# First attention: runs of 320 keys in the traded softmax weights, and another order of their transfers

## The reference, cut to what matters

```
q = (latents @ Wq)                       # latents: layernorm(x), 4 batches x 256 rows
k, v = concat([ctx, latents]) @ Wk, Wv   # 1601 + 256 = 1857 keys, 4 key heads, 8 query heads share one
scores = einsum('bqhgd,bkhd->bhgqk', q, k) / sqrt(128)
attn   = softmax(scores)
out    = einsum('bhgqk,bkhd->bqhgd', attn, v)   # then @ Wo
```

## Time and profile before

| | |
|---|---|
| median of 3 runs | 3167.3 us (3165.0 to 3168.3) |
| the profiled execution, its own time | 3163.8 us |
| its span in the profile | 3162.1 us |
| busy share of the span | PE 95%, PEld 84%, DVE 66%, ACT 56%, POOL 28% |
| granted PE clock, mean | 0.983 |
| softmax part of the first attention | about 545 to 2086 us of the span |

### The profile page before, as it was taken

The page is one execution under the profiler, slowest core; times in us unless marked ns, Lnnn a source line. Parts: engine busy times, 40 slices in busy tenths (PEclk is TensorE's granted clock), DMA queues, the critical chain, the costliest instruction groups (busy, mean ns, idle before and its releaser), DMA issues. The chain is left out here.

```text
span 3162.1 us, 53842 instructions
## 1 busy us (share of the span) xinstructions
PE 3008.4 (95%) x18405; PEld 2670.3 (84%) x18405; DVE 2076.8 (66%) x3217; ACT 1761.0 (56%) x3357; POOL 889.4 (28%) x725
## 2 busy tenths in 40 slices
PE   8999998999999999999999999979979899999886
PEld 8888887799999999899998999978857788888675
DVE  3333333688888888788887888864454466667576
ACT  3322344566766666666666666652243466556363
POOL 0000121344444444344444444442200021111234
PEclk9999999899999999999999999999989899999999
DMA  7665595776777767677767777546746511110387
GB/s 250 215 217 200 200 294 204 146 161 160 164 163 157 162 159 162 152 162 159 160 157 158 159 161 158 138 130 232 237 161 229 182 30 41 33 35 28 124 302 263
DMA packets 395364, 522.17 MB, mean 165 GB/s; under 512 B 35356, under 2 KB 292684, under 8 KB 395112
## 3 DMA queue, kind: packets, MB, share of 16 engines
q1 hardware_dynamic: 392552, 510.57, 59.2%
q0 software_dynamic: 2560, 8.39, 0.8%
HBM read 238.15 MB, written 146.46 MB: 122 GB/s over the span
## 5 line engine op out<-in xcount | busy, mean ns | idle before, releaser
L707 POOL TENSOR_TENSOR a_t_lo<-a_turned,a_t_hi 128x512 fp32r<-128x512 f32 x512 | 648.8, 1288 | 941.4 <-ACT a_t_hi L836 941.4
L827 ACT ACTIVATE a_probs<-a_ps_s,a_neg_max 128x1024 f32<-128x1024 f32 (+1 forms) x512 | 529.3, 1034 | 476.4 <-DVE a_neg_max L879 473.6
L872 DVE TENSOR_REDUCE a_half_max<-a_ps_s 128x1 f32<-128x1024 f32 (+1 forms) x512 | 570.7, 1115 | 191.1 <-PE a_ps_s L724 186.9
L722 PE MATMUL a_ps_s<-a_k_buf,a_q_buf 128*128 128x512 f32 (+1 forms) x1024 | 420.6, 411 | 18.0 <-ACT a_probs L827 11.8
L723 PE MATMUL a_ps_s<-a_k_buf,a_q_buf 128*128 128x512 f32 (+1 forms) x1024 | 386.6, 378 | 0.0
L724 PE MATMUL a_ps_s<-a_k_buf,a_q_buf 128*128 128x512 f32 (+1 forms) x1024 | 385.5, 376 | 0.0
L908 DVE TENSOR_TENSOR a_x_lo<-a_ps_x,a_x_hi 128x512 fp32r<-128x512 f32 (+1 forms) x512 | 314.2, 614 | 107.4 <-ACT a_x_hi L845 107.4
L454 DVE TENSOR_TENSOR p_out<-p_ps_j,p_out 128x512 fp32r<-128x512 f32 (+3 forms) x196 | 153.0, 780 | 327.4 <-ACT p_out L383 327.4
L898 DVE STREAM_TRANSPOSE a_turned<-xn 128x512 f32<-128x512 f32 x512 | 357.5, 698 | 1.5 <-POOL a_t_lo L707 1.5
L383 ACT ACTIVATE p_out<-p_ps_j 128x512 fp32r<-128x512 f32 (+3 forms) x196 | 142.1, 725 | 340.2 <-PE p_ps_j L288 340.2
L722 PE MATMUL a_ps_o<-a_t_hi,a_v_buf 128*128 128x256 f32 x1024 | 298.8, 292 | 5.6 <-issue 3.0
(11 more groups left out here) (383 smaller groups left out, 7001.1 us busy)
## 6 DMA issues: line engine op xcount, KB each, us to landing
xn<-a_probs SPq DMA_DIRECT2D x1024, 128.0 KB, 3.4
a_q_all<-p_out SPq DMA_DIRECT2D x64, 512.0 KB
a_q_buf<-a_q_all SPq DMA_DIRECT2D x128, 256.0 KB, 3.3
a_k_buf<-a_k_all SPq DMA_DIRECT2D x64, 464.5 KB, 4.0
a_v_all<-p_out SPq DMA_DIRECT2D x56, 512.0 KB
d_w_raw<-e_wt_all SPq DMA_DIRECT2D x31, 768.0 KB, 5.8
a_k_all<-p_out SPq DMA_DIRECT2D x48, 384.0 KB
a_v_buf<-a_v_all SPq DMA_DIRECT2D x64, 256.0 KB
```

Source lines behind the costliest of these rows:

```text
L707: pool.tensor_tensor(t_lo[:, slot, :, :], turned[:, slot, :, :], t_hi[:, slot, :, :].bitcast(F32), ALU.subtract).then_inc(t_done, 1)
L722: pe.matmul(o, w_hi, m_hi, start=first, stop=False)
L827: act.activation(probs[j][u.a][:, lo:hi], s_flat[:, lo:hi], ACT.Exp, bias=neg_max[:, j:j + 1], scale=SCALE, accum_out=half_sum[:, bass.ds( ...
L872: dve.reduce_max(half_max[:, half:half + 1], s_flat[:, lo:hi], AX.X).then_inc(max_done, 1)
```

## The change

The runs of a trade grow from 256 to 320 keys, so that 1280 keys are turned and 577 are plain. That makes five turned pairs and three plain groups (two of four transposes, one of two with 65 rows). The rings become 5 and 3. The second set of `traded` becomes a buffer of its own, `traded1`; the first stays in `xn`. The fourth run now reaches into the second half of the exponential, so its transfer waits for that too; the four transfers are issued in the order first, third, second, fourth. On each engine the fifth turned pair takes a place in the written order that a plain group had, or one next to it. The loads of values keep their number, with other sizes.

```diff
-    RUN = 256
+    RUN = 320
     TURNED = RUNS * RUN
...
-    RING, PRING, XBANKS = 4, 4, 2
+    RING, PRING, XBANKS = 5, 3, 2
...
-            traded = xn[:, :, :].rearrange("p t d -> p (t d)")[:, 0:2 * QT * TURNED].rearrange("p (a j g r) -> p a j g r", a=2, j=QT, g=RUNS)
+            traded = [xn[:, :, :].rearrange("p t d -> p (t d)")[:, 0:QT * TURNED].rearrange("p (j g r) -> p j g r", j=QT, g=RUNS),
+                      sb("traded1", [P, QT, RUNS, RUN])]
...
# SP, trade
-                    for c in range(RUNS):
-                        sp.dma_start(traded[SQ * c:SQ * (c + 1), u.a, j, :, :], probs[j][u.a][:, RUN * c:RUN * (c + 1)]
+                    for c in (0, 2, 1, 3):
+                        if c == RUNS - 1:
+                            sp.wait_ge(probs_done, 4 * u.n + 2 * j + 2)
+                        sp.dma_start(traded[u.a][SQ * c:SQ * (c + 1), j, :, :], probs[j][u.a][:, RUN * c:RUN * (c + 1)]
                                      ).then_inc(trade_done[j][u.a], 16)
...
# POOL, step
                     low(l, 3)
+                    low(l, 4)
                     low(w, 0)
...
# PE, step
                     weigh_turned(z, 2)
                     weigh_plain(z, 2)
                     turn_plain(l, 1)
-                    weigh_plain(z, 3)
+                    weigh_turned(z, 3)
                     scores(v, 0, 0)
                     turn_plain(l, 2)
                     scores(v, 0, 1)
-                    weigh_turned(z, 3, last=True)
-                    turn_plain(l, 3)
+                    weigh_turned(z, 4, last=True)
                     weigh_turned(l, 0, first=True)
                     weigh_plain(l, 0)
                     weigh_turned(l, 1)
...
# ACT, step
                     plain_high(w, 2)
                     exponentials(u, 0, 0)
-                    plain_high(w, 3)
+                    turned_high(w, 2)
                     exponentials(u, 0, 1)
-                    turned_high(w, 2)
                     turned_high(w, 3)
+                    turned_high(w, 4)
                     plain_high(v, 0)
...
# DVE, turn_traded and step
-                                  traded[:, u.a, :, :, 2 * SQ * p:2 * SQ * (p + 1)].rearrange("p j g (k r) -> p k (j g) r", k=2)
+                                  traded[u.a][:, :, :, 2 * SQ * p:2 * SQ * (p + 1)].rearrange("p j g (k r) -> p k (j g) r", k=2)
...
                     turn_traded(l, 3)
                     maximum(v, 1, 0)
-                    plain_low(l, 3)
+                    turn_traded(l, 4)
                     maximum(v, 1, 1)
                     negate_maximum(v, 1)
                     plain_low(w, 0)
```

More of the change, by code:

```diff
@@ L526, in grouped_attention_block @@
     VPIECES = sum(len(p) for p in VALUE_PIECES)
-    assert QT == 2 and len(CHUNKS) == 4 and HPG == 8 and TURNED <= 2 * BANK and TBLOCKS % 2 == 0 and WIDTH % 2 == 0
+    assert QT == 2 and len(CHUNKS) == 4 and HPG == 8 and (RUNS - 1) * RUN <= 2 * BANK and TPAIRS == 5 and PPAIRS == 3 and TBLOCKS % 2 == 0 and WIDTH % 2 == 0
     assert PLAIN % 2 == 1 and TPAIRS * HEADS % RING == 0 and PPAIRS * HEADS % XBANKS == 0 and PPAIRS * HEADS % PRING == 0
```

## The result

The changed kernel takes 3224.4 us (median; 3221.5 to 3228.3), 1.0185 [1.0168, 1.0202] of the time before: 57 us slower, where 11 us faster was forecast. The profiled execution took 3228.3 us, its span is 3226.6 us.

A forecast was written before the change was run, and what follows sets the result against it. Bound: a chain of scores, maxima, negation, exponential in the loop (96 units), PE in the first batch (32). Loop -2.9 us, first batch -8.3 us, sum -11 us: 3156 from the median 3167.3; range 3136 to 3172, the forecast's own 3146 to 3163.

The forecast's parts named there:

- rival B: Whole kernel: PE is the bound, so 56 us go, to 3111; chance 0.05.
- C: Rival: DVE's fifth transpose costs nothing between S1 and S0; 3134; chance 0.12.
- that cover: Between S0 and S1, PE reaches the weighings 0.1 to 0.2 us after POOL's subtractions end; cost 0.
- S0 to S1: From first score weight load of query tile 0 (S0) to that of tile 1 (S1): 5.97 loop, 5.62 first batch.
- S1 to S0: From tile 1's first score weight load to the next unit's tile 0: 6.13 us loop, 6.05 first batch.
- the 0.06 us at S0: First batch: PE's slack at tile 0's first score load, absorbing 0.06 us of the transpose's added 0.19.
- Rival D: ACT's t_hi and x_hi hold up the exponential before S0; 4 to 20 us slower, 3171 to 3187; chance 0.17.
- one of the signs that the prediction named for its being wrong: The exponential before S0 is released by ACT's own copies and not by the negation.
- What costs nothing, and under what: POOL, ACT, SP and transfers: cost 0, ACT at worst 0.1 us a unit, though SP's trade is released 2.9 us later.
- The ten us: Slack of the traded data: DVE needs them only at the end of its next step, some ten us later.
- The share: Busy share of the DMA engines: goes from 70% to about 80%.
- Rival E: Larger, later trades make DVE's first-pair transpose wait; each 0.1 us costs 13 us, 0.2 us makes 3182; chance 0.04.

The follow-up runs named there:

- full engines with the early release: Kernel before, first three of the four transfers carrying 320 elements a row instead of 256, rows at a distance of 320: 3169.0 us.
- the late release with short rows: Kernel before, a unit's last DVE transpose moved behind the first maximum of tile 1, the 65-row subtraction ahead of it: 3197.4 us, 1.0095.
- early transpose: Changed kernel, transfers in natural order, DVE's fifth transpose moved ahead of the first maximum of tile 1: 3154.7 us, 0.9955.
- only SP is held: Kernel with the early transpose, SP holding a unit's first trade until DVE has done the first maximum of tile 1: 3184.9 us, 1.0057.
- the best version: Early transpose kernel, queries ahead of second trade, PE's last transposes behind tile 0's second score half, `turn_traded(l, 1)` ahead of `plain_low(l, 1)`: 3136.9 us, 0.9906.

## Why the prediction was wrong, point by point

**What bounds the kernel: right.** A chain in the loop, PE in the first batch. With 0.44 us less work for PE a unit, the clean loop unit fell by 0.06 us, not by 0.44; rival B is out, and so is C: the transpose was not free (below). What showed it was the 0.06 us between the accumulator read and the next weight load; the weight loads' share was 92% in both stretches of the earlier trace rows, where PE set the pace and where the chain did, and does not tell them apart. No wait of PE for POOL shows in the changed kernel's waits, so that cover held.

**The chain terms: right, to a few hundredths.** The clean pieces, all 20th percentiles like the clean unit: S0 to S1 5.61 in the first batch (forecast 5.62) and 5.89 in the loop (5.97, reckoned from one unit at 6.19; the clean piece before was 6.10); S1 to S0 6.05 (6.05) and 6.08 (6.13). A clean unit of the loop, in the timeline of the changed kernel:

```profile
1157.31 0.19 PEld L726 LDWEIGHTS a_ps_s<-a_k_buf,a_q_buf 128*128 128x128 f32 x1 [0.31 <-ACT a_probs L830]
...
1160.15 0.70 DVE L901 STREAM_TRANSPOSE a_turned<-xn 128x512 f32<-128x512 f32 x1
...
1160.78 0.99 DVE L875 TENSOR_REDUCE a_half_max<-a_ps_s 128x1 f32<-128x833 f32 x1
...
1160.89 0.63 ACT L839 ACTIVATE a_t_hi<-a_turned 128x512 fp32r<-128x512 f32 x1 [1.66 <-DVE a_turned L901]
1160.93 2.49 SPq L649 DMA_DIRECT2D xn<-a_probs  x4
...
1161.43 0.58 ACT L848 ACTIVATE a_x_hi<-a_ps_x 128x512 fp32r<-128x512 f32 x1
...
1161.80 0.21 DVE L882 TENSOR_SCALAR a_neg_max<-a_half_max 128x1 f32<-128x1 f32 x1
...
1162.14 1.12 ACT L830 ACTIVATE a_probs<-a_ps_s,a_neg_max 128x1024 f32<-128x1024 f32 x1
...
1163.15 0.19 ACT L830 ACTIVATION_READ_ACCUMULATOR a_probs<-a_ps_s,a_neg_max  x1
...
1163.40 0.19 PEld L726 LDWEIGHTS a_ps_s<-a_k_buf,a_q_buf 128*128 128x128 f32 x1
```

The second maximum of tile 1 starts 3.47 us after S1, as forecast, against 3.28 in the earlier trace rows; S0 follows at 6.09, 0.06 us after the accumulator read's end. The transpose put 0.15 us on this piece: moved away it falls from 6.08 to 5.93.

In the first batch the forecast wanted 0.06 us behind the accumulator read at both instants. The timeline there has it at S1 only:

```profile
740.66 0.19 ACT L830 ACTIVATION_READ_ACCUMULATOR a_probs<-a_ps_s,a_neg_max 128x1 f32 x1
740.97 0.19 PEld L726 LDWEIGHTS a_ps_s<-a_k_buf,a_q_buf 128*128 128x128 f32 x1
...
746.37 0.19 ACT L830 ACTIVATION_READ_ACCUMULATOR a_probs<-a_ps_s,a_neg_max 128x1 f32 x1
746.61 0.19 PEld L726 LDWEIGHTS a_ps_s<-a_k_buf,a_q_buf 128*128 128x128 f32 x1
```

0.12 us at S0 (740.97), 0.05 at S1. So the 0.06 us at S0 were no slack that goes. The clean piece grew from 5.91 to 6.05, by 0.14, as in the loop by 0.15 (5.93 to 6.08); the forecast's 0.19 less 0.06 came to the same by luck.

**Rival D: a tie, with no price to be seen.** In the clean unit ACT's two copies end at 1162.01, and so does the negation; the exponential has no idle time in front of it. So one of the two exponentials of a unit has left the wait for the negation (96 times, where before there were 197), one of the signs that the prediction named for its being wrong. But the piece is no longer than 6.13: the mechanism is there, at the edge, and did not set the time.

**The step that failed: "What costs nothing, and under what", its sentences on SP and the transfers.** It saw that SP's trade is released 2.9 us later, which is what was measured (3.62 us after S1 instead of 0.75), and set it against the traded data, with some ten us to spare, alone. Four things were wrong in it.

- *The ten us.* They hold for the first trade of a unit: it lands 10.9 us before DVE needs it in the kernel before, 7.4 in the changed one. The second trade had 5.7 us, and 1.6 are left (medians); DVE waited 11 times for traded data, 11.2 us in all.
- *The share.* It scaled with bytes, to 80%. Measured: 94 to 98%.
- *What stands behind.* Each queue that a step is moved past counts, and the queries' load is the last in SP's step. The prediction named no load behind the trade, and this one came late: it landed 6.5 us after issue, and up to 10.5. Rival E had the mechanism's direction, the wrong load, and a chance of 0.04.
- *The product.* Either half alone is cheap: full engines with the early release (3169), the late release with short rows (11 us beyond its chain). Together they cost 70 us of late units, some 20 of them by the lower clock behind PE's holes, for which the sum had no term. The prediction priced each alone, at nothing.

The release accounts for 37 of the 55 us between late and early transpose (27.3 to 64.5 where only SP is held). The other 18 lie with the 0.6 us that this hold was short of, or with the transpose's own place on DVE; no run separates these. Part of both sums is the clock: it is low in 3 units with the early transpose, in 6 with SP held and in 12 of the changed kernel, and by the division above that makes 6.7, 11.1 and 20.9 us.

## What to carry to other kernels

Before a release of transfers is moved later, list what the same queue issues behind them, with the slack of each: the last small load pays for the whole burst. Don't scale the busy share of DMA engines by bytes (here a quarter more in three of four transfers took it from 0.72 to 0.92), and price "more bytes" and "later start" together. An operation that releases a queue belongs in the slack ahead of a wait, not behind it: here one line moved was worth 74 us, 19 of them the chain's. And before an operation is moved off a chain, look at what wait it fills where it stands: the four transposes filled 0.35 us of PE's.

## What was unexpected of the hardware

The time of a packet of the trade grows faster than its bytes. Mean ns of a packet and share of the DMA engines, evaluated from the packet records of the trace between 1000 and 1200 us, in kernels with one order of work on all engines:

| bytes per packet | mean ns | share | query load, median us to landing |
|---|---|---|---|
| 1024 (before) | 73 | 0.72 | 3.3 |
| 1152 | 87 | 0.82 | 3.5 |
| 1280 | 111 | 0.92 | 4.2 |
| 1536 | 147 | 1.05 | 7.1 |

A quarter more bytes take half as long again. At the start of a burst, with nothing else under way, a packet of 1024 takes 46 to 49 ns and one of 1280 55 to 58, about in proportion; so what grows is what overlapping transfers cost each other. The share is the packets' time by the time of the 16 engines, and at 1.05 packets of one engine must overlap in it. My reading, which no run tests by itself, is that a high share is in part waiting; 92% could be had at no price. So the share is not a bound by itself. Nor is the landing time alone: in the best version the queries land 6.7 us after issue, later than the 6.5 of the changed kernel, and nobody waits, because they are issued some 13 us ahead of S0 instead of 8. What counts is the landing against the moment of need.
